# A soft mixture-of-experts tail: one tanh group moved ahead of an exponential, the combine product turned to 336 columns, the last logits stored slot by slot

## The chip, the cores and the metric

One Trainium2 chip, one of its cores. The metric is the device time of one execution in microseconds (us): three runs of the kernel before gave 433.04, 431.68 and 431.97, a median of 431.97 us. Everything is in float32, or in float32 split into two parts where a product is marked fp32r.

## The reference

Eight batches of 56 tokens (448 in all) of width 128. First a cross attention over 1500 context rows with 16 heads, then a soft mixture of experts with 64 experts of 32 slots each (2048 slots):

```python
x = x + xattn(layernorm(x), ctx, Wq, Wk, Wv, Wo)      # softmax over 1500 rows, 16 heads of 64
u = layernorm(x)
logits = (einsum('tzd,ed->tze', u, phi_w) + phi_b).reshape(8, 56, 64, 32)   # expert n, slot p
D = softmax(logits, axis=3)                           # dispatch: over the 32 slots of an expert
C = softmax(logits, axis=2)                           # combine: over the 64 experts of a slot
X = clip(einsum('tznp,tzd->npd', D, u), -33000, 65000)
X = tanh((X - mean(X)) * rsqrt(var(X) + 1e-5))
Y = einsum('npd,ndH->npH', X, expert_w) + expert_b[:, None, :]
x = x + einsum('tznp,npH->tzH', C, Y)
```

The einsum for `X` sums over all tokens. No expert's input is complete before the dispatch weights of every token are.

## The kernel before

The kernel is written with an engine program each for TensorE (PE), VectorE (DVE), ScalarE (ACT), GpSimd (POOL) and the DMA issuer SyncE (SP). Each engine runs its instructions in the order in which they are written, and waits on semaphores where the code says `wait_ge`. No scheduler moves anything.

The 448 tokens are four pairs of batches of 112 tokens (`q` = 0 to 3, `LAST` = 3). Attention takes most of the run. The softmaxes of pairs 0 to 2 are worked in beside it. The tail, some 50 us long, holds what needs the last pair.

The 2048 slots stand as 16 blocks of 128 (`k`, four experts each), and the tail walks through them in four quarters (`r`). The stages of a quarter are these:

- `slots_in`: PE adds up the experts' inputs of the quarter in a PSUM bank.
- `slot_stats` (DVE) clips and takes mean and variance. `slot_root` (POOL, four small instructions) makes the scale and the offset. `tanh_slots` (ACT) applies them.
- `turn_xt` (PE) transposes the quarter, `copy_xtT` (ACT) copies it out. `experts` (PE, 16 small products) multiplies by the expert weights. `add_expert_bias` (DVE) adds the bias and writes `yt`.
- `combine(0, r)` (PE) multiplies the turned combine weights `combT` of pairs 0 to 2 by `yt`: for each block three products, with the weights of one pair (112 columns) stationary and `yt` (128 columns) moving. `combine(1, r)` does the same for the last pair, after all else.

Between them stands the combine softmax of the last pair, which has its own chain. ACT copies the logits out of PSUM (`copy_logits`). DVE takes the maximum over the experts (`combine_max`). POOL subtracts it from the lower 32 experts, DVE from the upper 32 (`combine_shift_upper`). ACT takes the exponential of all 2048 columns (`combine_exp(LAST)`). DVE sums in two halves (`combine_sum_part`), takes the reciprocal and scales quarter by quarter (`combine_scale_quarter`). PE transposes (`turn_comb(LAST)`) and ACT copies to `combT`.

The logits of a token are stored with the slots innermost: column 32n + s for expert n and slot s. A maximum or a sum over the experts of one slot therefore reads with a step of 32 elements (128 bytes).

In the printed code below `by_expert` shapes the 2048 columns as 64 experts x 32 slots, `by_slot` as 32 x 64 with that step. `bank(k)` is one of the eight PSUM banks, `RING` the four through which transposes go. `tr` is a transpose on PE.

Of the kernel before, what the change touches and what calls it, by code (L numbers as in the profile page):

```python
# [5 lines left out]
F32 = mybir.dt.float32  # L6
# [6 lines left out]
def xattn_softmoe_kernel(  # L13
# [61 lines left out]
    with ExitStack() as ctx:  # L75
# [118 lines left out]
        comb = logit  # L194
        stats_at = [stat0_at, stat1_at, t0_at + KB8, t0_at + KB8 + 384]
# [10 lines left out]
        yt = at("yt", [128, NS, H], F32, t0_at)  # L206
        out_sb = at("out_sb", [PT, NQ, D], F32, oT_at + 2048)
# [123 lines left out]
        y2_pe = sem("y2_pe")  # L331
        out_dve = sem("out_dve")
# [92 lines left out]
        def _(pool):  # L425
# [121 lines left out]
            def combine_shift(q, n0=0, n1=N_EXP):  # L547
                pool.wait_ge(cmax_dve, q + 1)
                if q == LAST:
                    pool.wait_ge(last_dsub, LC)  # L550
# [72 lines left out]
            combine_shift(LAST, 0, N_EXP // 2)  # L623
# [5 lines left out]
        def _(pe):  # L629
# [381 lines left out]
            def turn_comb(q):  # L1011
                if q < LAST:
                    pe.wait_ge(comb_pool, q + 1)
                for r in range(4):
# [9 lines left out]
                    for c in range(4):  # L1024
                        k = 4 * r + c
                        last = tr(bank(RING[r])[:, PT * c:PT * c + PT], comb[q][:, 128 * k:128 * k + 128],
# [64 lines left out]
            def combine(part, r):  # L1091

                pe.wait_ge(yt_dve, max(r, part) + 1)
                q0, q1 = PARTS[part]
                for k in range(4 * r, 4 * r + 4):
                    for q in range(q0, q1):
                        last = mm(bank(SLOT_BANKS[part])[0:PT, H * (q - q0):H * (q - q0) + H],  # L1097
                                  combT[:, k, PT * q:PT * q + PT], yt[:, k, :],
                                  start=(k == 0 and q == q0), stop=(k == NS - 1), skip_group_check=True)
                if r == 3:  # L1100
                    last.then_inc(y2_pe, 1)

# [5 lines left out]
            combine(0, 0)  # L1108
            turn_xt(2)
            combine(0, 1)  # L1110
            experts(2)
            turn_xt(3)
            combine(0, 2)
            experts(3)
            turn_comb(LAST)
            combine(0, 3)
            for r in range(4):
                pe.wait_ge(combT_act, 12 + r + 1)
                combine(1, r)
# [3 lines left out]
        def _(act):  # L1123
# [68 lines left out]
            def copy_logits(q, c):  # L1192
                act.wait_ge(logit_pe, LC * q + c + 1)
                if q == LAST:
                    act.wait_ge(last_dsub, c + 1)
                nc.scalar.copy(logit[q][:, 512 * c:512 * c + 512],
# [152 lines left out]
            copy_xtT(1)  # L1349
            combine_exp(LAST)  # L1350
            tanh_slots(2)
# [3 lines left out]
            copy_combT(LAST)  # L1355


        @block.vector
        def _(dve):
# [124 lines left out]
            def combine_max(q):  # L1484
                dve.wait_ge(logit_act, LC * (q + 1))
                v.tensor_reduce(cmax[q][:, :], by_slot(logit[q][:, :]), AX.X, ALU.max).then_inc(cmax_dve, 1)
# [10 lines left out]
            def combine_sum_part(q, part):  # L1497
# [4 lines left out]
                if part:  # L1502
                    dve.wait_ge(csum_part, 6 if q == LAST else 2 * (q + 1))
# [167 lines left out]
            def combine_shift_upper(q):  # L1671

                half_n = slice(N_EXP // 2, N_EXP)
                dve.wait_ge(cmax_dve, q + 1)
                v.tensor_tensor(by_expert(comb[q][:, :])[:, half_n, :], by_expert(logit[q][:, :])[:, half_n, :],
                                cmax[q][:, :].unsqueeze(1).broadcast_to([PT, N_EXP // 2, P_SLOT]),
                                ALU.subtract).then_inc(csub_dve, 1)

            def combine_scale_quarter(q, r):

                dve.wait_ge(crec_dve, q + 1)
                part = by_expert(comb[q][:, QUARTER * r:QUARTER * r + QUARTER])
                v.tensor_tensor(part, part, csum[q][:, :].unsqueeze(1).broadcast_to([PT, N_EXP // 4, P_SLOT]),
# [58 lines left out]
```

## Time and profile before

| | kernel before |
|---|---|
| median of three runs | 431.97 us |
| the profiled execution, its own time | 429.94 us |
| its span in the trace | 428.2 us |
| PE busy in the span | 417.8 us (98%) |
| DVE / ACT / POOL busy | 335.8 / 245.0 / 170.1 us |
| granted TensorE clock | full in all 40 slices |

The span runs from the first to the last recorded event. The other 1.74 us of the execution's own time lie around it. Times in the trace count from the span's start. A row of the timeline gives the start, the time until its last instruction ended, and how many instructions it merges. Where instructions overlap in an engine's pipeline, the next row begins before the last one has ended. What an instruction holds the engine for is then the distance between starts.

A PE product of float32 appears as two MATMUL records, a transpose as one. So the twelve products of a `combine(0, r)` are 24 records. PE is busy 98% of the span, yet the tail has gaps. A wait on PE there is what the change can touch.

### The profile page before, as it was taken

The numbers are of one execution on the slowest core, as the hardware profiler recorded it, in microseconds if no ns is written. First come the engines' busy times: TensorE is split into PE (matmuls) and PEld (weight loads), VectorE is DVE, ScalarE is ACT, GpSimd is POOL, SyncE is SP. The second block draws the span as 40 slices with busy tenths as digits, with TensorE's granted clock in tenths as the row PEclk, the third lists the DMA queues.
The fourth block names the chain that finished last, engine by engine and source line by source line (L and its number), as shares of the span: only waits on it lengthen the run. The fifth ranks groups of instructions, "written<-read, shape, count | busy, mean of one in ns | idle before, by whom it ended". The sixth has DMA issues, their size and how long they took to land.

```text
span 428.2 us, 7420 instructions
## 1 busy us (share of the span) xinstructions
PE 417.8 (98%) x2973; PEld 383.4 (90%) x2973; DVE 335.8 (78%) x615; ACT 245.0 (57%) x412; POOL 170.1 (40%) x99
## 2 busy tenths in 40 slices
PE   7999999999999999999999999999999999999897
PEld 5888999999999999889999998899999888999787
DVE  4788756776886778767898689978988899669981
ACT  3577547664664546654673766466655564645541
POOL 5419701424450405032608053617146543456710
PEclk9999999999999999999999999999999999999999
DMA  7410110213020011110020001001000000396000
GB/s 197 144 27 10 41 51 14 63 43 96 14 48 38 20 14 18 69 18 14 14 73 20 12 14 72 21 12 15 0 20 12 2 12 20 54 259 181 2 2 23
DMA packets 15418, 19.05 MB, mean 44 GB/s; under 512 B 4032, under 2 KB 10960, under 8 KB 15384
## 3 DMA queue, kind: packets, MB, share of 16 engines
q1 hardware_dynamic: 15384, 18.57, 17.0%
q8 instruction: 24, 0.39, 0.4%
q14 instruction: 10, 0.08, 0.2%
HBM read 18.31 MB, written 0.26 MB: 43 GB/s over the span
## 4 chain that ended last, share of the span: by engine, by line
PE 73%; DVE 17%; ACT 7%; DMA 1%; issue 1%; SPq 0%; ACTq 0%
PE turned L735 14%; PE acc L755 8%; PE acc L757 7%; PE acc L756 7%; PE scores L719 7%; PE scores L725 7%; PE scores L722 7%; DVE small L1411 5%; DVE pT_l L1421 4%; ACT prob L1167 4%; PE misc L772 3%; PE misc L641 2%; PE scores L1097 2%; ACT pT_h L1160 1%; PE misc L800 1%; ACT logit L1218 1%
## 5 line engine op out<-in xcount | busy, mean ns | idle before, releaser
L1160 ACT CAST pT_h<-turned 125x512 fp32r<-125x512 f32 x168 | 95.2, 590 | 123.6 <-PE turned L735 122.9
L1421 DVE TENSOR_TENSOR pT_l<-turned,pT_h 125x512 fp32r<-125x512 f32 x168 | 112.4, 686 | 56.7 <-ACT pT_h L1160 55.9
L1411 DVE TENSOR_REDUCE small<-scores 128x1 f32<-128x500 f32 x168 | 107.9, 673 | 3.7 <-PE scores L725 3.3
L735 PE MATMUL turned<-ident,prob 128*125 128x128 f32 x672 | 94.4, 276 | 2.0 <-DVE pT_l L1421 1.7
L735 PEld LDWEIGHTS turned<-ident,prob 128*125 128x125 f32 x672 | 87.5, 187 | 9.7 <-DVE pT_l L1421 3.9
L755 PE MATMUL acc<-pT_h,ctx_nh 125*128 125x256 f32 (+1 forms) x288 | 95.0, 330 | 0.0
L1167 ACT ACTIVATE prob<-scores,small 128x1500 f32<-128x1500 f32 x56 | 84.9, 1517 | 10.9 <-DVE small L1414 10.7
L757 PE MATMUL acc<-pT_h,ctx_nl 125*128 125x256 f32 (+1 forms) x288 | 86.5, 300 | 0.0
L756 PE MATMUL acc<-pT_l,ctx_nh 125*128 125x256 f32 (+1 forms) x288 | 86.4, 300 | 0.0
L719 PE MATMUL scores<-ctx_th,qk_h 128*128 128x500 f32 x168 | 70.3, 419 | 0.4 <-ACT prob L1167 0.4
L725 PE MATMUL scores<-ctx_th,qk_l 128*128 128x500 f32 x168 | 65.3, 389 | 0.0
L722 PE MATMUL scores<-ctx_tl,qk_h 128*128 128x500 f32 x168 | 65.0, 387 | 0.0
L755 PEld LDWEIGHTS acc<-pT_h,ctx_nh 125*128 125x128 f32 x288 | 54.6, 190 | 0.7 <-issue 0.5
L756 PEld LDWEIGHTS acc<-pT_l,ctx_nh 125*128 125x128 f32 x288 | 54.6, 190 | 0.6 <-issue 0.5
L757 PEld LDWEIGHTS acc<-pT_h,ctx_nl 125*128 125x128 f32 x288 | 54.4, 189 | 0.0
L444 POOL TENSOR_TENSOR ctx_nh<-ctx_raw,zero 125x1536 fp32r<-125x1536 f32 x8 | 22.0, 2746 | 60.9 <-PE acc L757 60.5
L719 PEld LDWEIGHTS scores<-ctx_th,qk_h 128*128 128x128 f32 x168 | 31.6, 188 | 7.4 <-issue 2.1
L725 PEld LDWEIGHTS scores<-ctx_th,qk_l 128*128 128x128 f32 x168 | 31.5, 188 | 6.5
L722 PEld LDWEIGHTS scores<-ctx_tl,qk_h 128*128 128x128 f32 x168 | 31.7, 189 | 5.9 <-issue 1.4
L551 POOL TENSOR_TENSOR logit<-logit,cmax 112x2048 f32<-112x2048 f32 (+1 forms) x4 | 16.1, 4030 | 34.0 <-DVE cmax L1482 32.5
L448 POOL TENSOR_TENSOR ctx_nl<-ctx_raw,ctx_nh 125x1536 fp32r<-125x1536 f32 x8 | 28.0, 3497 | 0.6
L462 POOL TENSOR_TENSOR qk_h<-ahead,zero 128x896 fp32r<-128x896 f32 x6 | 10.1, 1680 | 30.7 <-PE scores L725 17.2
(212 smaller groups left out, 552.5 us busy)
## 6 DMA issues: line engine op xcount, KB each, us to landing
ctx_raw<-in_ctx_dram SPq DMA_DIRECT2D x7, 750.0 KB
rbc<-rden_row SPq DMA_DIRECT2D x15, 128.0 KB, 3.5
rbc<-rden_row SPq DMA_DIRECT2D x8, 192.0 KB, 3.0
eb<-in_L_ffn_expert_b_dram SPq DMA_DIRECT2D x4, 256.0 KB, 6.0
ctx_raw<-in_ctx_dram SPq DMA_DIRECT2D x3, 224.0 KB, 5.3
wq_sb<-in_L_xattn_Wq_dram SPq DMA_DIRECT2D x2, 256.0 KB, 4.6
wk_sb<-in_L_xattn_Wk_dram SPq DMA_DIRECT2D x2, 256.0 KB, 5.3
wv_sb<-in_L_xattn_Wv_dram SPq DMA_DIRECT2D x1, 512.0 KB, 3.6
```

What stands on the lines that cost most here:

```text
L448: gp.tensor_tensor(ctx_nl[a][:, :, :], ctx_raw[:, :, :], ctx_nh[a][:, :, :].bitcast(F32), ALU.subtract).then_inc(ctx_nat, 1)
L719: mm(o, hi, ctx_th[a][:, keys], start=True, stop=False)
L722: mm(o, hi, ctx_tl[a][:, keys], start=False, stop=False)
L725: mm(o, lo, ctx_th[a][:, keys], start=False, stop=True).then_inc(scores_pe, 1)
L735: last = tr(turned[0:CK, m, 128 * c:128 * c + 128], prob[u][:, CK * j:CK * j + CK], ident[:, :])
L755: mm(o, ctx_nh[a][:, j, :], hi, start=(j == 0), stop=False)
L756: mm(o, ctx_nh[a][:, j, :], lo, start=False, stop=False)
L757: last = mm(o, ctx_nl[a][:, j, :], hi, start=False, stop=(j == NC - 1))
L1160: nc.scalar.copy(pT_h[0:CK, PLACES[g // NT % 2][t], CPB * k:CPB * k + CPB, :], turned[0:CK, (KB * u + k) % 2, :].rearrange("p (c r) -> p c ...
L1167: nc.scalar.activation(prob[u][:, :].rearrange("p (k w) -> p k w", k=KB), scores[:, :, 0:KW], ACT.Exp, bias=negmax[:, u:u + 1], accum_out= ...
L1411: m = v.tensor_reduce(bankmax[:, u, k:k + 1], scores[:, k, 0:KW], AX.X, ALU.max)
L1421: v.tensor_tensor(pT_l[0:CK, place, dst, :], turned[0:CK, (KB * u + k) % 2, :].rearrange("p (c r) -> p c r", c=CPB), pT_h[0:CK, place, dst ...
```

## The change

It has four parts.

1. The logits of the last pair are stored by slot: column 64s + n instead of 32n + s. `copy_logits` writes with a step of 64 elements. The maximum, the two shifts and the sum then run along contiguous experts. Sum and maximum are one instruction each. The scaling reads with the step of 64 and writes the old order into `disp3`, from which PE transposes. POOL's shift loses its wait on `last_dsub`.
2. On ACT, `tanh_slots(2)` comes before `combine_exp(LAST)`. On DVE, `add_expert_bias(0)` comes before the upper shift.
3. `combine(r)` has `yt` stationary and the weights of three pairs (336 columns) moving: one product for each block instead of three. Its result is transposed, so an ACT copy to `y2T` and three PE transposes into bank M1 follow. The first three pairs' addition and store wait for them.
4. `combine_last` runs as `combine(1, r)` did. The three transposes stand between its second and third quarter.

```diff
-                nc.scalar.copy(logit[q][:, 512 * c:512 * c + 512], bank(...)[0:PT, :])   # q == LAST
+                    dst = logit[q][:, :].rearrange("p (s n) -> p n s", n=N_EXP)[:, EPB * c:EPB * c + EPB, :]
+                    src = bank(LOGIT_BANKS[q][c])[0:PT, :].rearrange("p (n s) -> p n s", s=P_SLOT)
+                    nc.scalar.copy(dst, src).then_inc(logit_act, 1)
...
+            def last_combine_shift_lower():
+                half_n = slice(0, N_EXP // 2)
+                by_slot = comb[LAST][:, :].rearrange("p (s n) -> p s n", n=N_EXP)[:, :, half_n]
+                pool.wait_ge(cmax_dve, LAST + 1)
+                gp.tensor_tensor(by_slot, by_slot, cmax[LAST][:, :].unsqueeze(2).broadcast_to([PT, P_SLOT, N_EXP // 2]),
+                                 ALU.subtract).then_inc(csub_pool, 1)
...
-                for k in range(4 * r, 4 * r + 4):
-                    for q in range(q0, q1):
-                        last = mm(bank(SLOT_BANKS[part])[0:PT, H * (q - q0):H * (q - q0) + H],
-                                  combT[:, k, PT * q:PT * q + PT], yt[:, k, :], ...)
+                for k in range(4 * r, 4 * r + 4):
+                    last = mm(bank(S0)[:, 0:LAST * PT], yt[:, k, :], combT[:, k, 0:LAST * PT],
+                              start=(k == 0), stop=(k == NS - 1))
...
+            def turn_y2():
+                pe.wait_ge(y2T_act, 1)
+                for q in range(LAST):
+                    last = tr(bank(M1)[0:PT, D * q:D * q + D], y2T[:, PT * q:PT * q + PT], ident[:, :])
+                last.then_inc(y2turn_pe, 1)
...
-            for r in range(4):
-                pe.wait_ge(combT_act, 12 + r + 1)
-                combine(1, r)
+            combine_last(0)
+            combine_last(1)
+            turn_y2()
+            combine_last(2)
+            combine_last(3)
...
+            act.wait_ge(y2_pe, 1)
+            nc.scalar.copy(y2T[:, :], bank(S0)[:, 0:LAST * PT]).then_inc(y2T_act, 1)
...
+                v.tensor_reduce(cmax[LAST][:, :], slot_rows(logit[LAST][:, :]), AX.X, ALU.max)     # one, contiguous
+                v.tensor_reduce(csum[LAST][:, :], slot_rows(comb[LAST][:, :]), AX.X, ALU.add)      # one, contiguous
+                src = comb[LAST][:, :].rearrange("p (s n) -> p n s", n=N_EXP)[:, EPB * r:EPB * r + EPB, :]
+                v.tensor_tensor(by_expert(comb_by_expert[LAST][:, QUARTER * r:QUARTER * r + QUARTER]), src,
+                                csum[LAST][:, :].unsqueeze(1).broadcast_to([PT, EPB, P_SLOT]), ALU.mult)
```

The order on ACT in the tail, from the tanh of the second quarter on (`logit_101` is the last pair's logits, which become its combine weights). Before:

```order
L1339 ACTIVATE xt<-xt,xt_nb,xt_rs 128x128 [waits nb_pool]
L1339 ACTIVATE xt<-xt,xt_nb,xt_rs 128x128 x3
L1344 COPY xtT<-turned 128x512 [waits xtT_pe] x2
L1218 ACTIVATE logit_101<-logit_101 112x2048 [waits csub_dve,csub_pool]
L1339 ACTIVATE xt<-xt,xt_nb,xt_rs 128x128 [waits nb_pool]
L1339 ACTIVATE xt<-xt,xt_nb,xt_rs 128x128 x3
L1344 COPY xtT<-scores 128x512 [waits xtT_pe]
```

And now:

```order
L1368 ACTIVATE xt<-xt,xt_nb,xt_rs 128x128 [waits nb_pool]
L1368 ACTIVATE xt<-xt,xt_nb,xt_rs 128x128 x3
L1373 COPY xtT<-turned 128x512 [waits xtT_pe] x2
L1368 ACTIVATE xt<-xt,xt_nb,xt_rs 128x128 [waits nb_pool]
L1368 ACTIVATE xt<-xt,xt_nb,xt_rs 128x128 x3
L1247 ACTIVATE logit_101<-logit_101 112x2048 [waits csub_dve,csub_pool]
L1373 COPY xtT<-scores 128x512 [waits xtT_pe]
```

The exponential of 2048 columns stands behind the third tanh group now, but still ahead of the copy of that quarter's transpose.

On DVE, from the third quarter's statistics to the scaling. Before:

```order
L1663 BN_AGGR xt_mv<-xt_st 128x2 x3
L1675 TENSOR_TENSOR logit_101<-logit_101,cmax_112 112x1024 [waits cmax_dve]
L1668 TENSOR_TENSOR yt<-scores,eb 128x512 [waits yt_pe,eb_in]
L1668 TENSOR_TENSOR yt<-acc,eb 128x512 [waits yt_pe]
...
L1500 TENSOR_REDUCE cmax_112<-logit_101 112x32 [waits cexp_act]
L1500 TENSOR_REDUCE half_stat<-logit_101 112x32 [waits cexp_act]
L1504 TENSOR_TENSOR cmax_112<-cmax_112,half_stat 112x32 [waits csum_part]
L1506 RECIPROCAL cmax_112<-cmax_112 112x32 [waits csum_dve]
L1668 TENSOR_TENSOR yt<-misc,eb 128x512 [waits yt_pe]
L1683 TENSOR_TENSOR logit_101<-logit_101,cmax_112 112x512 [waits crec_dve] x4
```

And now:

```order
L1703 BN_AGGR xt_mv<-xt_st 128x2 x3
L1708 TENSOR_TENSOR yt<-scores,eb 128x512 [waits yt_pe,eb_in]
L1715 TENSOR_TENSOR logit_101<-logit_101,cmax_112 112x32x32 [waits cmax_dve]
L1708 TENSOR_TENSOR yt<-acc,eb 128x512 [waits yt_pe]
...
L1524 TENSOR_REDUCE cmax_112<-logit_101 112x32 [waits cexp_act]
L1526 RECIPROCAL cmax_112<-cmax_112 112x32 [waits csum_dve]
L1708 TENSOR_TENSOR yt<-misc,eb 128x512 [waits yt_pe]
L1722 TENSOR_TENSOR disp_104<-logit_101,cmax_112 112x512 [waits crec_dve] x4
```

The first bias addition has passed the upper shift, the sum is one instruction, and the scaling writes `disp_104` (`disp3`).

On PE, the end of the program. Before:

```order
L1097 MATMUL scores<-yt,combT 112x128 [waits yt_dve]
L1097 MATMUL scores<-yt,combT 112x128 x11
L1097 MATMUL acc<-yt,combT 112x128 [waits yt_dve,combT_act]
L1097 MATMUL acc<-yt,combT 112x128 x3
L1097 MATMUL acc<-yt,combT 112x128 [waits yt_dve,combT_act]
L1097 MATMUL acc<-yt,combT 112x128 x3
L1097 MATMUL acc<-yt,combT 112x128 [waits yt_dve,combT_act]
```

And now:

```order
L1105 MATMUL scores<-combT,yt 128x336 [waits yt_dve]
L1105 MATMUL scores<-combT,yt 128x336 x3
L1114 MATMUL acc<-yt,combT 112x128 [waits combT_act]
L1114 MATMUL acc<-yt,combT 112x128 x3
L1114 MATMUL acc<-yt,combT 112x128 [waits combT_act]
L1114 MATMUL acc<-yt,combT 112x128 x3
L1123 MATMUL misc<-ident,y2T 112x128 [waits y2T_act]
L1123 MATMUL misc<-ident,y2T 112x128 x2
L1114 MATMUL acc<-yt,combT 112x128 [waits combT_act]
```

Twelve products of 128 columns have become four of 336, and three transposes stand inside the last pair's combine.

## Rows read from the trace of the kernel before

**Rows 1.** Chain that ended last, tail: start us, us, what.
```profile
405.42 1.91 ACT logit L1218
407.33 1.55 ACT xt L1339 x4
...
412.27 1.05 PE misc L1087 x32
...
413.35 0.70 DVE yt L1668
...
414.09 2.88 PE scores L1097 x24
...
417.98 0.92 PE turned L1026 x8
...
425.81 0.29 DVE out_sb L1712
```
**Rows 2.** Timeline, PE: start us, us, line, operation, count [idle before].
```profile
402.69 1.08 PE L1087 MATMUL scores<-ew,xtT 128*32 128x128 f32 x32
...
409.02 0.63 PE L1078 MATMUL scores<-ident,xt 128*128 128x128 f32 x4 [0.16 <-ACT xt L1339]
409.48 2.79 PE L1097 MATMUL scores<-yt,combT 128*112 128x128 f32 x24
```
**Rows 3.** Timeline, DVE, 398 to 406 us.
```profile
398.07 3.72 DVE L1486 TENSOR_REDUCE cmax<-logit 112x32 f32<-112x2048 f32 x1
401.71 0.69 DVE L1655 TENSOR_SCALAR xt<-misc 128x512 f32<-128x512 f32 x1
...
403.63 1.69 DVE L1675 TENSOR_TENSOR logit<-logit,cmax 112x1024 f32<-112x1024 f32 x1
405.25 0.68 DVE L1668 TENSOR_TENSOR yt<-scores,eb 128x512 f32<-128x512 f32 x1
405.85 0.67 DVE L1668 TENSOR_TENSOR yt<-acc,eb 128x512 f32<-128x512 f32 x1
```
**Rows 4.** Timeline, POOL, 398 to 406 us.
```profile
398.37 0.24 POOL L566 TENSOR_SCALAR xt_nb<-xt_mv 128x4 f32<-128x4 f32 x1
...
400.09 0.20 POOL L571 TENSOR_TENSOR xt_nb<-xt_nb,xt_rs 128x4 f32<-128x4 f32 x1
401.87 2.37 POOL L551 TENSOR_TENSOR logit<-logit,cmax 112x1024 f32<-112x1024 f32 x1 [1.58 <-DVE cmax L1486]
404.33 1.09 POOL L566 TENSOR_SCALAR xt_nb<-xt_mv 128x4 f32<-128x4 f32 x1
```
**Rows 5.** Groups by line and shape: count | busy us, mean ns | idle before.
```profile
L1472 DVE TENSOR_REDUCE dmax<-logit 112x32 f32<-112x1024 f32 x4 | 4.7, 1207 | 0.0
L1478 DVE TENSOR_REDUCE cmax<-logit 112x32 f32<-112x1024 f32 x2 | 4.0, 1976 | 0.0
...
L1683 DVE TENSOR_TENSOR logit<-logit,cmax 112x512 f32<-112x512 f32 x4 | 2.5, 683 | 0.0
...
L1506 DVE RECIPROCAL cmax<-cmax 112x32 f32<-112x32 f32 x2 | 0.7, 354 | 0.1
...
L531 POOL TENSOR_TENSOR disp<-logit,dmax 112x2048 f32<-112x2048 f32 x3 | 10.9, 3648 | 23.7 <-DVE dmax L1472 23.7
```
**Rows 6.** Groups by line and shape, PE: eight float32 products of 512 columns.
```profile
L800 PE MATMUL misc<-phiT,xnT 128*112 128x512 f32 x16 | 8.2, 592 | 0.0
```
**Rows 7.** Timeline, ACT, 387 to 393 us.
```profile
387.09 0.63 ACT L1212 ACTIVATE disp<-disp 112x512 f32<-112x512 f32 x1 [2.80 <-DVE disp L1526]
387.63 0.57 ACT L1196 COPY logit<-turned 112x512 f32<-112x512 f32 x1
...
392.71 0.63 ACT L1212 ACTIVATE disp<-disp 112x512 f32<-112x512 f32 x1 [1.05 <-DVE disp L1526]
```
**Rows 8.** DMA issues of the output: count, KB, us from issue to landing.
```profile
out_dram<-out_sb SPq DMA_DIRECT2D x1, 168.0 KB, 2.6
...
out_dram<-out_sb SPq DMA_DIRECT2D x1, 56.0 KB, 1.6
```

More of the change, by code:

```diff
@@ L331, in xattn_softmoe_kernel @@
         y2_pe = sem("y2_pe")
+        y2T_act = sem("y2T_act")
+        y2turn_pe = sem("y2turn_pe")
         out_dve = sem("out_dve")
@@ L1025, in turn_comb @@
                         k = 4 * r + c
-                        last = tr(bank(RING[r])[:, PT * c:PT * c + PT], comb[q][:, 128 * k:128 * k + 128],
+                        last = tr(bank(RING[r])[:, PT * c:PT * c + PT], comb_by_expert[q][:, 128 * k:128 * k + 128],
                                   ident[0:PT, 0:PT])
@@ L1089, in experts, with combine, combine_last @@
                 last.then_inc(yt_pe, 1)
-            def combine(part, r):
-                pe.wait_ge(yt_dve, max(r, part) + 1)
-                q0, q1 = PARTS[part]
+            def combine(r):
+                pe.wait_ge(yt_dve, r + 1)
                 for k in range(4 * r, 4 * r + 4):
-                    for q in range(q0, q1):
-                        last = mm(bank(SLOT_BANKS[part])[0:PT, H * (q - q0):H * (q - q0) + H],
-                                  combT[:, k, PT * q:PT * q + PT], yt[:, k, :],
-                                  start=(k == 0 and q == q0), stop=(k == NS - 1), skip_group_check=True)
+                    last = mm(bank(S0)[:, 0:LAST * PT], yt[:, k, :], combT[:, k, 0:LAST * PT],
+                              start=(k == 0), stop=(k == NS - 1))
                 if r == 3:
                     last.then_inc(y2_pe, 1)
+            def combine_last(r):
+                pe.wait_ge(combT_act, 12 + r + 1)
+                for k in range(4 * r, 4 * r + 4):
+                    last = mm(bank(ACC)[0:PT, 0:H], combT[:, k, LAST * PT:TOK], yt[:, k, :],
+                              start=(k == 0), stop=(k == NS - 1))
+                if r == 3:
+                    last.then_inc(y2_pe, 1)
+            def turn_y2():
[3 more added lines that the diff above has]
+                last.then_inc(y2turn_pe, 1)
             pe.wait_ge(ew_in, 16)
@@ L1349, in _ @@
             copy_xtT(1)
+            tanh_slots(2)
             combine_exp(LAST)
-            tanh_slots(2)
             copy_xtT(2)
@@ L1482, in combine_max_part, with slot_rows, last_combine_max, last_combine_sum @@
                     v.tensor_tensor(cmax[q][:, :], cmax[q][:, :], half_stat[:, :], ALU.max).then_inc(cmax_dve, 1)
-            def combine_max(q):
-                dve.wait_ge(logit_act, LC * (q + 1))
-                v.tensor_reduce(cmax[q][:, :], by_slot(logit[q][:, :]), AX.X, ALU.max).then_inc(cmax_dve, 1)
+            def slot_rows(ap):
+                return ap.rearrange("p (s n) -> p s n", n=N_EXP)
+            def last_combine_max():
+                dve.wait_ge(logit_act, LC * (LAST + 1))
+                v.tensor_reduce(cmax[LAST][:, :], slot_rows(logit[LAST][:, :]), AX.X, ALU.max).then_inc(cmax_dve, 1)
+            def last_combine_sum():
+                dve.wait_ge(cexp_act, LAST + 1)
+                v.tensor_reduce(csum[LAST][:, :], slot_rows(comb[LAST][:, :]), AX.X, ALU.add).then_inc(csum_dve, 1)
+                dve.wait_ge(csum_dve, LAST + 1)
+                v.reciprocal(csum[LAST][:, :], csum[LAST][:, :]).then_inc(crec_dve, 1)
             def dispatch_sum(q, part):
@@ L1502, in combine_sum_part @@
                 if part:
-                    dve.wait_ge(csum_part, 6 if q == LAST else 2 * (q + 1))
+                    dve.wait_ge(csum_part, 2 * (q + 1))
                     v.tensor_tensor(csum[q][:, :], csum[q][:, :], half_stat[:, :], ALU.add).then_inc(csum_dve, 1)
```

52 lines of the change are left out of this document (26 added, 26 removed).

## The prediction

> **What bounds the kernel now.** I read the chain of waits first, from 400 us to the end. It holds what the end waits for: PE from 409.02 us on, broken once by the third bias addition, and ahead of that ACT and DVE [rows 1, 2]. Only the tail is changed, so only the tail can pay. The chain's middle is the place to look at. The exponential of the combine weights runs 405.42 to 407.33, and only then the third tanh group (1.55 on the chain), for which PE waits until 409.02 [rows 1, 2]. From there PE has work behind work: combine, experts, four transposes, and one more gate. The third bias addition (413.35, 0.70) must end before the third combine quarter can start at 414.09 [rows 1]. That start, which I call the gate, is the coordinate of my sum. Behind it stand two combine quarters of the first three pairs, one experts quarter, the sixteen transposes of the last weights and the last pair's combine, whose end releases DVE at 425.81 [rows 1]. Whatever moves the gate, or what is shorter behind it, moves the end by as much, if nothing else becomes late.
>
> Second I read the timelines of DVE and POOL from 398 to 406 us, since they feed that gate. DVE's maximum holds it from 398.07 to 401.71, 3.64 us. POOL's shift starts after it at 401.87 and takes 2.37, and DVE's upper shift takes 1.69 [rows 3, 4]. The first bias addition starts at 405.25, though its experts were done at 402.69 + 1.08 = 403.77 [rows 2, 3]. It stood behind the upper shift on DVE.
>
> **Part 1, the layout.** A maximum over 1024 columns takes 1.207 us where they are contiguous, 1.976 with the step of 128 bytes [rows 5]. 2048 columns took 3.72 with the step [rows 3], so a column costs (3.72 - 1.976)/1024 = 1.70 ns there. A contiguous column costs at most 1.207/1024 = 1.18 ns, and 0.95 if the fixed part of the strided rows (1.976 - 1.744 = 0.23) is taken off; I take 1.04, between them. The contiguous maximum then takes 1.207 + 1024 x 1.04 ns = 2.28, holding DVE for 2.20: from 398.07 to 400.27. Bounds: 2.1 and 3.64. Statistics of the third quarter hold DVE for 403.63 - 401.71 = 1.92 [rows 3] and end at 402.2. DVE then waits for the first experts. Their end does not move, since PE, ACT and POOL ahead of them are unchanged. The first bias addition starts at 403.77 + 0.08 = 403.85.
>
> From there DVE is the chain:
> - first bias addition, 405.85 - 405.25 = 0.60 [rows 3]: to 404.45;
> - upper shift. 512 columns of such a subtraction or product take 0.683 [rows 5]; 1024 take that plus 512 x 1.04 ns = 1.22. Before it took 1.69, but POOL's shift ran until 404.24 [rows 4], and from there to DVE's end at 405.32 [rows 3] it is 1.08. I take 1.15; bounds 1.08 and 1.69: to 405.60;
> - second bias addition 0.60: to 406.20;
> - statistics of the last quarter 1.92, plus the 0.09 until their last end: 408.21;
> - POOL's root. In the profile it runs 398.37 to 400.29 [rows 4], 1.92, and starts some 0.2 behind the statistics: 2.14: 410.35;
> - the tanh group 1.64 and 0.05 to start: 412.04; PE 0.14 later: 412.18;
> - PE's four transposes hold it 409.48 - 409.02 = 0.46 [rows 2]: the gate at 412.64.
>
> It stood at 414.09, so the gate moves by -1.45. PE itself would be ready earlier. Its first combine quarter can start at about 404.65, behind the second experts, and with 2.26 for a quarter (below), 0.46 for transposes and 1.0 for experts it is free at 410.7. PE idles some 1.4 us there, and the work is not late.
>
> The copies of the logits get a step of 256 bytes on ACT's writes. No row shows a strided write on ACT. Bounds: the 0.57 of now [rows 7], and 0.57 + 512 x (1.70 - 1.04) ns = 0.91 if ACT suffers as DVE does. I take 0.75. All of that is covered. Each copy starts 0.54 behind its exponential [rows 7], and with c for a copy the fourth exponential could start at 387.63 + 3c + 2 x 0.54, which passes its 392.71 [rows 7] only for c above 1.33.
>
> The Trainium skill ("Advanced Engine Details and Errata", SBUF Cachelines) says that an access of another 16-byte line each time pays a penalty. By this rule the change buys its contiguous reductions with steps in five other places, the four scalings and the copies; for DVE's reads the trace agrees, 1.976 against 1.207.
>
> The scalings read with the step now. Each held DVE some 0.60 of its 0.683 [rows 5]; with 512 x 0.66 ns more, 0.95. Four of them, from about 411.7, end at 415.5. PE wants the first when its third combine and fourth experts are over, at 412.64 + 2.26 + 1.05 = 415.95. They are covered, with 0.45 us to spare for the last and more for the ones before. Without that cover every 0.1 us on each would cost 0.4.
>
> **Part 2, the order.** The tanh group now needs POOL's root of the third quarter. POOL's shift starts at 400.45 (0.08 behind the maximum's end at 400.37) and now subtracts one value for 32 contiguous columns, as the dispatch shift does: 3.648 for 2048 columns, 1.9 for 1024; the row of the same half now says 2.37 [rows 4, 5]. Both bounds stay. The root follows by 1.92 + 0.09 and ends at 404.36 or 404.83. DVE's upper shift starts at 404.45. This is a race. POOL's small instruction at 404.33 took 1.09 where its like took 0.24, exactly while DVE had its own upper shift [rows 4, 3]. If POOL loses, the root ends at about 405.9.
>
> The Trainium skill ("SBUF — State Buffer", Who interferes with whom) calls it an exclusive lock between a DVE instruction with two SBUF inputs and a GpSimd one that reads SBUF. By this rule the loser stands still for the whole 1.15, and the trace agrees with 1.09 against 0.24.
>
> If POOL wins, tanh ends at 406.0, the exponential at 407.9, and DVE, busy with statistics until 408.2, sums (2.20), inverts (0.354 and 0.05, [rows 5]) and adds the third bias at 410.9, behind the experts. It is not late. If POOL loses: tanh to 407.6, exponential 1.91 [rows 1] to 409.45, sum to 411.65, reciprocal to 412.05, third bias to 412.8, gate 412.84. The loss is 0.2. The exponential hides behind the statistics in the one case and is nearly late in the other.
>
> **Part 3, 336 columns.** Twelve products are 24 records in 2.79, a record lasting about 0.275: (2.79 - 0.275)/23 = 0.109 from start to start, 2.62 a quarter [rows 2]. Records of 512 columns come in pairs that last 2 x 8.2/16 = 1.02, one of them 0.592 [rows 6]: 0.43 from start to start. So 336 columns: 0.109 + 208 x (0.43 - 0.109)/384 = 0.283. Eight records: 2.26. The saving is 0.36 a quarter; bounds 0 (the wide product brings nothing) and 0.5 (against the 2.88 of [rows 1]). Two quarters stand behind the gate: -0.72. The three transposes cost 3 records at about 0.92/8 = 0.115 [rows 1]: +0.33. Their copy (336 columns, less than the 0.57 of 512 [rows 7]) lies under two quarters of the last pair's combine, 1.75 us.
>
> **Sum.** -1.45 - 0.72 + 0.33 = -1.84 if POOL wins, -1.64 if it loses. I take -1.75. Against the profiled execution: 429.94 - 1.75 = 428.2. The median of the runs is 431.97, 2.03 above it, and I carry the difference over to it: 430.2.
>
> **The stores.** The first store is released by the transposes now, and leaves some 0.2 ahead of where it stood; the second leaves 1.8 earlier. A whole combine of the last pair stood between them, 32 records at 0.109, 3.5 us, and the first landed within 2.6 [rows 8]. Now it is half of that, 1.75, and the first is still in flight when the second leaves. In the sum the second keeps its 1.6.
>
> **Rivals.**
> - *The locks cost more.* POOL's shift takes 2.37 and DVE's upper shift 1.69: the gate stands 0.5 later and the loss of the race is added, -1.84 + 0.7 = -1.14: 430.8. For: both rows stand so today. Against: they were measured while colliding with each other, which the new order takes apart. Chance 0.10.
> - *The wide product is no cheaper*: PE is 2.62 a quarter whatever the shape. -1.84 + 0.72 = -1.12: 430.85. For: no float32 row of 336 columns. Against: [rows 6]. Chance 0.08.
> - *The second store waits for the first.* It lands 2.6 after its issue instead of 1.6: -0.75: 431.2. For: three times the bytes ahead of it. Against: the small store's 1.6 is mostly a fixed time, and the bigger one needs only 1.0 more. Chance 0.10.
> - *The layout does nothing*: contiguous sums of this shape cost as strided ones. The sum of the weights then starts at 409.5 and holds 3.7, and the gate stands at 414.35: +0.26 - 0.72 + 0.33 = -0.1: 431.85. Against: [rows 5]. Chance 0.04.
> - *Slower: ACT's strided writes.* A copy taking c above 1.33 delays the fourth exponential by 3c - 4.0, and all of the tail with it. At c = 1.9 the gain is gone; at 2.6 (5 ns a column) it is +3.8 - 1.75 = +2.05: 434.0. For: no row has such a write. Against: DVE's strided reads cost 1.7 ns a column, a third of it. Chance 0.07.
>
> **How the numbers follow.** Forecast 0.61, the rivals 0.39 together. A difference of 0.3% is 1.3 us, about what a measurement of this kernel can tell from no change. The forecast's own values, -1.64 to -1.84, stand only 0.4 from that line, and I give 0.04 of its 0.61 to the near side. Faster: 0.57, 0.03 of the locks, and 0.02 of the stores, 0.62. Same: 0.04 + 0.07 + 0.08 + 0.08 + 0.04 = 0.31. Slower: 0.07. The range: downward the unknowns are the wide product's 0.5 and a start of PE at 410.7 instead of 412.2, with scatter of the runs of 0.3: 429.0. Upward it takes in locks, product, stores and layout: 431.8. Outside lie the strided write and some 0.08 below.
>
> **What would show it.** The maximum at 2.3 us and the sum likewise, without a strided one. The first bias addition at 403.85. The last tanh group at 410.4, PE waiting for it by 1.2 to 1.5 us, and its next combine quarter at 412.6. The wide records 0.28 apart. The logits copies under 0.95. The last output addition at 424.0. I am wrong if the gate stands elsewhere because the exponential or a lock is on the chain, or if a logits copy takes over 1.33.

## The result and the profile after

| | before | after |
|---|---|---|
| median of 13 runs each | 431.39 us | 428.93 us |
| ratio, 95% interval | | 0.9943 (0.9927 to 0.9958) |
| profiled execution, own time / span | 429.94 / 428.2 us | 429.79 / 428.0 us |
| first score product in the trace | 11.74 us | 13.57 us |
| first slot statistics in the trace | 394.31 us | 396.17 us |
| first slot statistics to the span's end | 33.89 us | 31.83 us |

The change made the kernel faster by 0.57%, 2.46 us between the medians; the interval spans 1.8 to 3.15 us. I had forecast 1.75 us, 430.2 us, in a range from 429.0 to 431.8. The median lies 0.07 us below the range. The interval holds 2.0 us as well as 2.46, and 1.75 lies just outside it.

The two spans, 428.2 and 428.0, hide the gain. This execution of the changed kernel started badly. Its first score product came 1.83 us later than that of the kernel before, and it carried the delay to the tail (1.86 us). The chain of its first microseconds shows what happened (start us, us, what):

```profile
2.64 5.44 DMA ctx_raw<-in_ctx_dram
8.08 0.14 issue
8.21 0.92 PE misc L651 x4
9.14 0.51 PE turned L679
...
9.87 0.21 PE turned L679
...
13.57 0.49 PE scores L729
```

The kernel before, same view:

```profile
2.64 4.77 DMA ctx_raw<-in_ctx_dram
...
8.48 0.11 PE turned L669
...
11.74 0.49 PE scores L719
```

The context landed 0.67 us later, and then each product of two weight blocks (L679, before L669) took 0.21 where it had taken 0.10 to 0.11. The busy time by stretches of the changed kernel's profile (us, PE, PEld, DVE, ACT, POOL busy, then PEclk, DMA share, GB/s) gives the reason:

```profile
0.00:8.00 8.00, 4.41 (x15) 3.10 (x15) 2.40 (x12) 1.87 (x2) 3.62 (x12) 1.00 0.69 198
8.00:12.00 4.00, 3.79 (x24) 3.07 (x25) 1.79 (x4) 1.17 (x2) 3.02 (x3) 0.57 0.74 194
12.00:16.00 4.00, 3.99 (x25) 3.32 (x25) 2.87 (x6) 1.75 (x4) 3.92 (x2) 1.00 0.58 183
```

The first stretch of the kernel before, same view:

```profile
0.00:8.00 8.00, 5.25 (x19) 3.52 (x19) 2.78 (x13) 1.87 (x2) 3.52 (x12) 1.00 0.75 204
```

The granted clock was 0.57 on average from 8 to 12 us, so TensorE ran at the lower of its two levels, 1.2 GHz, for most of it. Ahead of it PE had been busy 4.41 of 8 us, where it was busy 5.25 in the kernel before, whose clock stayed at 1.00. Such a start isn't a property of the change: 9 of the 72 runs of the kernel before that were made beside the experiments have a mean clock of 0.996 to 0.998 too, the mean of this profile being 0.996.

The tail must therefore be read from a mark of its own. I take the first slot statistics on DVE. The mark in the kernel before, and in the changed kernel:

```profile
394.31 0.63 DVE L1655 TENSOR_SCALAR xt<-scores 128x512 f32<-128x512 f32 x1
...
396.17 0.63 DVE L1695 TENSOR_SCALAR xt<-scores 128x512 f32<-128x512 f32 x1
```

The timeline of the changed kernel's tail (start us, us, engine, line, operation):

```profile
399.93 2.25 DVE L1520 TENSOR_REDUCE cmax<-logit 112x32 f32<-112x2048 f32 x1
...
402.26 1.92 POOL L562 TENSOR_TENSOR logit<-logit,cmax 112x1024 f32<-112x1024 f32 x1
...
405.76 0.69 DVE L1708 TENSOR_TENSOR yt<-scores,eb 128x512 f32<-128x512 f32 x1 [1.66 <-PE scores L1097]
405.98 0.20 POOL L581 TENSOR_TENSOR xt_nb<-xt_nb,xt_rs 128x4 f32<-128x4 f32 x1
406.21 1.65 ACT L1368 ACTIVATE xt<-xt,xt_nb,xt_rs 128x128 f32<-128x128 f32 x4 [0.98 <-POOL xt_nb L581]
406.37 1.22 DVE L1715 TENSOR_TENSOR logit<-logit,cmax 112x1024 f32<-112x1024 f32 x1
...
407.77 1.90 ACT L1247 ACTIVATE logit<-logit 112x2048 f32<-112x2048 f32 x1
...
410.02 2.25 DVE L1524 TENSOR_REDUCE cmax<-logit 112x32 f32<-112x2048 f32 x1
410.19 0.23 POOL L576 TENSOR_SCALAR xt_nb<-xt_mv 128x4 f32<-128x4 f32 x1 [4.01 <-DVE xt_mv L1703]
...
412.14 1.65 ACT L1368 ACTIVATE xt<-xt,xt_nb,xt_rs 128x128 f32<-128x128 f32 x4 [2.01 <-POOL xt_nb L581]
...
413.42 3.92 DVE L1722 TENSOR_TENSOR disp<-logit,cmax 112x512 f32<-112x512 f32 x4
...
413.94 0.63 PE L1088 MATMUL scores<-ident,xt 128*128 128x128 f32 x4 [1.19 <-ACT xt L1368]
...
414.40 2.43 PE L1105 MATMUL scores<-combT,yt 128*128 128x336 f32 x8
...
416.76 1.08 PE L1097 MATMUL misc<-ew,xtT 128*32 128x128 f32 x32
...
419.36 2.44 PE L1105 MATMUL scores<-combT,yt 128*128 128x336 f32 x8
421.63 1.91 PE L1114 MATMUL acc<-yt,combT 128*112 128x128 f32 x16
...
425.65 0.29 DVE L1754 TENSOR_TENSOR out_sb<-x_sb,acc 112x128 f32<-112x128 f32 x1 [1.19 <-PE acc L1114]
```

The maximum takes 2.25 us where it took 3.72 [rows 3], POOL's shift 1.92 where it took 2.37 [rows 4]. The upper shift takes 1.22 where it took 1.69 [rows 3]; that is the order's doing and not the layout's, since it takes 1.22 in the kernel with the order only, too. DVE waits 1.66 for the first experts. The third combine quarter starts at 414.40, 18.23 us behind the mark; before it was 414.09 - 394.31 = 19.78 [rows 1]. PE waits 1.19 us for the last tanh group.

### The profile page after: what moved, and what is told of

Its sections match the earlier page's. It is cut to its first block, busy times and chain, and to the rows that moved or that the text cites. A ratio compares the mean times of both kernels' runs of the same rounds, so it can differ in the third digit from the quotient of the medians.

```text
span 428.0 us, 7292 instructions
## 1 busy us (share of the span) xinstructions
PE 417.5 (98%) x2912; PEld 380.0 (89%) x2912; DVE 333.5 (78%) x613; ACT 247.1 (58%) x413; POOL 168.8 (39%) x99
## 4 chain that ended last, share of the span: by engine, by line
PE 73%; DVE 16%; ACT 7%; DMA 1%; POOL 1%; issue 1%; SPq 0%; POOLq 0%; DVEq 0%
PE turned L745 14%; PE acc L765 8%; PE acc L767 7%; PE acc L766 7%; PE scores L729 7%; PE scores L735 7%; PE scores L732 7%; DVE small L1442 5%; DVE pT_l L1452 4%; ACT prob L1192 4%; PE misc L782 3%; PE misc L651 2%; ACT pT_h L1185 1%; PE misc L810 1%; DMA ctx_raw<-in_ctx_dram 1%; PE scores L1105 1%
## 5 line engine op out<-in xcount | busy, mean ns | idle before, releaser
L553 POOL TENSOR_TENSOR logit<-logit,cmax 112x2048 f32<-112x2048 f32 x3 | 13.8, 4588 | 32.5 <-DVE cmax L1513 32.5
```

## The experiments

Each kernel with an interval ran 6 to 12 times, on the same chip as the kernel before, whose medians beside them were 431.44 (first four kernels of the table), 431.18 (next four) and 431.34 us (last). The other two have a single run each, so only their traces are used. The last column is the time from the first slot statistics to the end of the span, which I call the tail. The trace gives spans to 0.1 us, so a tail is good to 0.05.

| kernel | median us | ratio (95% interval) | tail us |
|---|---|---|---|
| before again | 431.31 | 1.0004 (0.9986 to 1.0021) | 33.87 |
| change again | 428.82 | 0.9942 (0.9919 to 0.9964) | 31.87 |
| wide product only | 430.55 | 0.9970 (0.9952 to 0.9989) | 33.10 |
| layout and order only | 429.66 | 0.9951 (0.9933 to 0.9969) | 32.23 |
| order only | 433.12 | 1.0045 (1.0021 to 1.0070) | 35.46 |
| layout only | 430.01 | 0.9970 (0.9947 to 0.9992) | 32.18 |
| change with the old order | 428.67 | 0.9939 (0.9917 to 0.9962) | 31.20 |
| change, logits copied twice | 430.00 | 0.9969 (0.9949 to 0.9988) | 31.89 |
| change, exponential first (ACT) | 429.47, one run | | 33.56 |
| change, upper shift first (DVE) | 430.32, one run | | 31.34 |
| old order, second quarter split | 428.27 | 0.9938 (0.9921 to 0.9955) | 30.91 |

**Both kernels again.** No edit.

> The kernel before, unchanged. It tells two places for the surplus of the measured change (-2.46 us of medians against -1.75 forecast and -2.02 between the first bias statistics and the last output addition of the two traces). Theory S (scatter of the start): the time from the first slot statistics to the end of the span is again 33.9 us within 0.1, and only the time before it differs from 394.31 us, by up to 2 us either way. Theory H (the head of the program is faster after the change, for instance through code loading): the head is longer here than in every run of changed kernels by some 0.4 us.

> The changed kernel, unchanged. Theory S: 31.8 us from the first slot statistics to the end of the span, within 0.1, against 33.9 before; its head falls among those of the kernel before; the medians of the same rounds differ by 2.0 us, give or take 0.6. Theory H: heads shorter by 0.4, medians 2.4 to 2.5 apart.

The tails came out at 33.87 and 31.87, within 0.04 of the first profiles. Read without the spans, from the mark to the start of the last output addition, the two pairs of traces differ by 31.50 - 29.48 = 2.02 and 31.51 - 29.50 = 2.01 us. From the first score product to the first slot statistics it took 382.57 and 382.60 us in the first pair of traces, 382.54 and 382.53 in the second. The head is the same in both programs, and only its start differs, at 11.6 to 13.6 us in these four. That is as theory S has it. The medians were again 2.5 us apart (431.31 and 428.82), more than the 2.0 of the tails, with an interval that still holds 2.0.

**The wide product alone.** It has parts 3 and 4 of the change on the kernel before. The diff is cut to the product.

```diff
...
-                    for q in range(q0, q1):
-                        last = mm(bank(SLOT_BANKS[part])[0:PT, ...], combT[:, k, PT * q:PT * q + PT], yt[:, k, :], ...)
+                    last = mm(bank(S0)[:, 0:LAST * PT], yt[:, k, :], combT[:, k, 0:LAST * PT], ...)
...
```

> Only the product of 336 columns, its copy, its transposes and the stores as changed; layout and order are those of before. My sum: the gate (start of the third combine quarter) stays 19.8 us behind the first slot statistics, each quarter of the first three pairs holds PE for 2.26 instead of 2.62, transposes cost 0.33: -0.4 us. Rival (a wide product is no cheaper): +0.33 us. Since the layout of before has a wait of PE on the third bias addition, the quarters ahead of it gain nothing.

The tail was 33.10, a gain of 0.78, twice my sum (0.73 at the start of the last output addition). The gate moved too: 413.42 against a mark of 394.00 is 19.42, 0.36 earlier. PE's own work stood ahead of the third bias addition there, so a shorter second combine brought the third experts, the bias and the gate forward. So the sentence of my expectation that the quarters ahead gain nothing was wrong. The rest is 0.34 and 0.36 for the two quarters less 0.33 for the transposes, as forecast for the change.

**Layout and order without the wide product.** The diff is cut as above.

```diff
...
-                    last = mm(bank(S0)[:, 0:LAST * PT], yt[:, k, :], combT[:, k, 0:LAST * PT], ...)
+                    for q in range(q0, q1):
+                        last = mm(bank(SLOT_BANKS[part])[0:PT, ...], combT[:, k, PT * q:PT * q + PT], yt[:, k, :], ...)
...
```

> Layout and order as changed, but twelve products of 128 columns a quarter and no transposes of the result, as before. My sum: the gate moves by the whole 1.45 to 1.55 us, and so does the end: -1.5 us. PE is busy 0.36 longer in each of the two quarters ahead of the gate, which its idle 1.2 us there covers. Rival (the wide product also pays ahead of the gate, by starting the third transposes sooner): only -1.2.

The tail was 32.23, a gain of 1.65. The gate stood 413.62 - 395.37 = 18.25 behind the mark, as in the change, so the wide product brings nothing ahead of it here. The other 0.1 lies in the quarter behind the gate. It held PE 2.71 (413.62 to 416.33) instead of 2.80 (414.09 to 416.89). The kernel before, behind its gate at 414.09 [rows 1]:

```profile
416.89 1.08 PE L1087 MATMUL misc<-ew,xtT 128*32 128x128 f32 x32
...
419.49 2.79 PE L1097 MATMUL scores<-yt,combT 128*112 128x128 f32 x24
422.12 3.66 PE L1097 MATMUL acc<-yt,combT 128*112 128x128 f32 x32
```

And this kernel, with its wait at the turn:

```profile
413.15 0.63 PE L1088 MATMUL scores<-ident,xt 128*128 128x128 f32 x4 [0.49 <-ACT xt L1353]
413.62 2.78 PE L1107 MATMUL scores<-yt,combT 128*112 128x128 f32 x24
```

Here a quarter whose first product waited for its operand is 0.09 slower, and with the layout the wait is at the turn, ahead of it.

**Order only.** The two swaps of the change on the kernel before.

```diff
+            tanh_slots(2)
             combine_exp(LAST)
-            tanh_slots(2)
...
-            combine_shift_upper(LAST)
             dve.wait_ge(eb_in, 16 * EPT)
             add_expert_bias(0)
+            combine_shift_upper(LAST)
```

> Only the order as changed (third tanh group ahead of the exponential on ACT, first bias addition ahead of the upper shift on DVE); layout by expert and twelve products as before. My sum: maximum still strided, so DVE comes to the first bias addition at 403.85 and to the upper shift at 404.45 (times of the profile of before); the root's small instructions meet the upper shift and end near 407.2, tanh to 408.9, exponential only then to 410.7, strided sums to 414.8, reciprocal 0.4, third bias addition 0.7: gate 415.8 instead of 414.09, so 1.7 us slower than before (35.6 us from the first slot statistics to the end). Rival (the order is worth something by itself, since the tanh group and the turn are earlier): some 0.5 us faster than before.

It was slower by 1.6 us in the tail (35.46, expected 35.6) and by 0.45% in the runs. The timeline shows the race lost and the exponential late:

```profile
404.55 1.22 DVE L1675 TENSOR_TENSOR logit<-logit,cmax 112x1024 f32<-112x1024 f32 x1
404.65 1.19 POOL L567 TENSOR_SCALAR xt_var<-xt_mv 128x4 f32<-128x4 f32 x1
...
408.84 1.90 ACT L1218 ACTIVATE logit<-logit 112x2048 f32<-112x2048 f32 x1
...
410.77 1.94 DVE L1500 TENSOR_REDUCE cmax<-logit 112x32 f32<-112x1024 f32 x1 [2.49 <-ACT logit L1218]
...
415.75 2.88 PE L1097 MATMUL scores<-yt,combT 128*112 128x128 f32 x24 [1.83 <-DVE yt L1668]
```

POOL's small instruction took 1.19 instead of 0.23 while DVE shifted. The exponential stood behind the tanh group, DVE waited 2.49 for it, and PE 1.83 for the third bias addition behind the sums. The rival, a gain of 0.5, did not occur.

**Layout only.** Here the old order of ACT and DVE stands on the new layout. The diff is against the kernel with layout and order.

```diff
-            tanh_slots(2)
             combine_exp(LAST)
+            tanh_slots(2)
...
             slot_stats(2)
+            last_combine_shift_upper()
             dve.wait_ge(eb_in, 16 * EPT)
             add_expert_bias(0)
-            last_combine_shift_upper()
```

> Only the layout as changed; order and products as before. My sum: the shorter maximum frees DVE at 400.3, the upper shift runs at 402.4 to 403.5 in the gap in which DVE otherwise waits for the first experts, the sum ends at 409.5, and the gate stands at 412.2 behind PE's own work and the third bias addition: 1.9 us faster than before, 32.0 us from the first slot statistics to the end, 0.2 better than layout and order together (32.23). Rival (the order is what brings the gain, as its place in the change suggests): the exponential ahead of the tanh group holds PE up, and the gain is under 1.0.

The tail was 32.18: 1.70 faster than before, 0.2 less than my sum, since the gate stood 414.52 - 396.42 = 18.10 behind the mark and not 412.2 - 394.31 = 17.89. It equals layout and order together (32.23). With the twelve products of 128 columns, the order brought nothing on top of the layout, and cost nothing.

**The change with the old order.** It is the same edit on the changed kernel.

> The changed kernel with the order of before on ACT and DVE: exponential ahead of the third tanh group, upper shift ahead of the first bias addition. My sum: gate at 411.75, two quarters shorter by 0.35 to 0.45 each, transposes 0.33: 2.8 us faster than before, 31.1 us from the first slot statistics to the end, 0.75 better than the change. Rival (the order carries the gain): slower than the change, 32.5 or more.

The tail was 31.20, 0.65 better than the change (31.85) and 0.1 from my sum. Its timeline:

```profile
402.55 1.24 DVE L1715 TENSOR_TENSOR logit<-logit,cmax 112x1024 f32<-112x1024 f32 x1
...
403.88 1.91 ACT L1247 ACTIVATE logit<-logit 112x2048 f32<-112x2048 f32 x1
...
404.30 0.69 DVE L1708 TENSOR_TENSOR yt<-scores,eb 128x512 f32<-128x512 f32 x1 [0.52 <-PE scores L1097]
...
411.45 0.69 DVE L1708 TENSOR_TENSOR yt<-misc,eb 128x512 f32<-128x512 f32 x1 [1.18 <-PE misc L1097]
411.55 0.63 PE L1088 MATMUL scores<-ident,xt 128*128 128x128 f32 x4 [0.17 <-ACT xt L1368]
...
412.20 2.53 PE L1105 MATMUL scores<-combT,yt 128*128 128x336 f32 x8
```

The upper shift fills the gap in which DVE waits for the first experts (0.52 is left of 1.66), and PE waits 0.17 for the last tanh group instead of 1.19. Between the medians the step is 0.15, which the runs cannot tell from nothing. The tails can: those of an unchanged kernel repeated within 0.04.

**Each logits copy twice.**

```diff
+                    nc.scalar.copy(spare, src)          # an unused place, the same step
                     nc.scalar.copy(dst, src).then_inc(logit_act, 1)
```

> The changed kernel with each of the four copies of the last logits made twice, first into an unused place with the same step. One copy holds ACT for 0.86 in the changed kernel. By my formula (a delay of 3c - 4.0 for c above 1.33) two of them, c = 1.72, delay the fourth exponential and the first slot statistics by 1.15 us, with nothing lost behind it: 1.1 slower than the change. Rival A (the copies are hidden wholly): no change. Rival B (they lie on the path all along): 4 x 0.86 = 3.4 slower, and then the change itself already loses 4 x 0.35 there.

In the changed kernel a copy holds ACT 390.34 - 389.48 = 0.86 (four exponentials in 394.57 - 388.94 = 5.63). The last part with the doubled copies:

```profile
388.75 0.63 ACT L1244 ACTIVATE disp<-disp 112x512 f32<-112x512 f32 x1 [2.81 <-DVE disp L1569]
389.29 1.05 ACT L1225 COPY junk<-turned 112x512 f32<-112x512 f32 x1
...
390.14 1.10 ACT L1226 COPY logit<-turned 112x512 f32<-112x512 f32 x1
...
395.54 0.65 ACT L1244 ACTIVATE disp<-disp 112x512 f32<-112x512 f32 x1
```

From the first to the fourth exponential it is 6.79, 1.16 more, and the tail behind the mark is unchanged at 31.89. The formula 3c - 4.0 holds: 1.15 was expected, and the medians, 430.00 and 428.82, lie 1.2 apart (1.4 if each is taken against its own kernel before, 431.18 and 431.44). The single strided copy, 0.86, stays under the 1.33 and costs nothing.

**Only ACT's order, only DVE's order.** One half of the edit above each, on the changed kernel.

> The changed kernel with the order of before on ACT alone: exponential ahead of the third tanh group, while the upper shift stays behind the first bias addition on DVE. My sum: the upper shift ends at 405.6 in the times of the profile of before, the exponential runs to 407.55, tanh to 409.1, the turn at 409.2, experts to 413.0, gate 413.8: 33.1 us from the first slot statistics to the end, against 31.85 for the change. Rival (the ACT order is what costs the change its 0.65 against the old order): 31.2.

> The changed kernel with the order of before on DVE alone: upper shift ahead of the first bias addition; tanh stays ahead of the exponential. My sum: the shift fills DVE's gap, statistics of the last quarter end 1.0 earlier, tanh no longer holds PE, but the exponential ends 1.3 later than with the old order, at 408.8, and with it the sum (411.1), reciprocal (411.5) and third bias addition: gate 412.25, 31.65 us. Rival (DVE's order alone carries the 0.65): 31.2.

The tails were 33.56 and 31.34. With the exponential first and the shift late, ACT holds the tanh group back behind a shift that is itself behind the bias addition, 1.7 worse than the change. I had expected 1.25 worse; the gate stands 413.96 - 394.14 = 19.82 behind the mark, expected 413.8 - 394.31 = 19.49. With the upper shift first, 0.5 of the 0.65 is had without touching ACT. I had expected 0.2 of it. The exponential was late, and DVE waited for it:

```profile
411.54 2.29 DVE L1524 TENSOR_REDUCE cmax<-logit 112x32 f32<-112x2048 f32 x1 [1.38 <-ACT logit L1247]
```

The sum starts 411.54 - 397.16 = 14.38 behind the mark, 1.45 later than with the old order on both engines (407.63 - 394.70 = 12.93). But there the third bias addition still waited 1.18 for the experts, and that wait covers most of it: the bias addition comes only 0.22 later (414.13 - 397.16 = 16.97 against 411.45 - 394.70 = 16.75).

**The version that follows.** Old order, and on PE half of the second combine quarter behind the third experts. The diff is cut to PE.

```diff
...
             turn_xt(2)
-            combine(1)
+            combine(1, 0, 2)
             experts(2)
+            combine(1, 2, 4)
             turn_xt(3)
...
```

> The change with the old order on both engines, and the second combine quarter in two halves around the third experts on PE: two blocks before them cover the copy, two behind them cover the third bias addition, for which PE idles 0.2 to 0.3 and starts slowly in the version with the old order (31.20 us). My sum: PE without a gap to the third combine quarter, 0.4 us better: 30.8 us from the first slot statistics to the end, 3.1 us faster than the kernel before. Rival (the experts then wait for the copy of their transpose, 0.8 us behind the turn, since half a quarter, 1.13 us, covers it only barely): no better than 31.2.

```profile
407.83 1.30 PE L1105 MATMUL scores<-combT,yt 128*128 128x336 f32 x4
409.06 1.08 PE L1097 MATMUL misc<-ew,xtT 128*32 128x128 f32 x32
...
410.07 1.40 PE L1105 MATMUL scores<-combT,yt 128*128 128x336 f32 x4
410.21 0.69 DVE L1709 TENSOR_TENSOR yt<-misc,eb 128x512 f32<-128x512 f32 x1
...
411.43 0.63 PE L1088 MATMUL scores<-ident,xt 128*128 128x128 f32 x4
...
411.90 2.43 PE L1105 MATMUL scores<-combT,yt 128*128 128x336 f32 x8
```

PE has no gap from the third turn to the third combine, and the third bias addition lies under the second half. The half quarter behind the experts took 1.40 and the one ahead of them 1.30, though no wait is shown before it. So the slow start of a quarter doesn't need a wait. The tail is 30.91, 0.94 better than the change and 2.96 better than before. The median, 428.27, is the lowest of all, but its interval overlaps those of the change and of its old-order twin.

## Why the prediction was wrong

The mechanisms were right and the sum was too small: 1.75 us, where the two pairs of traces give 2.02 and 2.01 behind the mark (2.06 and 2.00 with the rounded spans), and the medians 2.46.

- **The maximum and the first bias addition.** 2.20 us of hold were forecast, 402.10 - 399.93 = 2.17 came. The bias addition starts 405.76 - 396.17 = 9.59 behind the mark, forecast 403.85 - 394.31 = 9.54.
- **The chain to the gate.** The upper shift held DVE 1.13 (forecast 1.15), statistics 1.92. Behind them I charged POOL's root 2.14, and it ended 2.00 behind the statistics. In the row that I took it from, POOL had still been busy with the root of the quarter ahead, and started 0.22 behind the statistics; free, it starts 0.08 behind them. The gate moved by 1.55 instead of 1.45. This is the one term of it that was mis-sized.
- **The wide product.** 2.26 a quarter were forecast, and the second of the two came in 2.27. The first held PE 416.76 - 414.40 = 2.36, but it had been 2.80 before and not 2.62. The 0.09 of a quarter behind a wait went with the wait; I had named the 2.88 as a bound and summed without it. Both 2.26 and 2.62 are also about 0.1 too low for a quarter that experts follow (2.36 in the change, 2.71 with layout and order only). That this cancels in the difference is luck.
- **The race.** POOL's root ended at 406.18, DVE's upper shift started at 406.37. POOL won by 0.19, where I saw 0.09 (404.45 - 404.36). Halving the loss cost the forecast another 0.1.
- **The transposes** cost 0.33, as forecast, and their copy was hidden. **The stores**: the first landed within 2.2 us, the second within 1.6. That rival did not occur.
- **ACT's strided writes.** 1.03 to 1.06 us were measured, above my upper bound of 0.91. I had taken DVE's cost of a strided read for ACT's write. They stayed under the limit of 1.33 by their hold of 0.86, and the doubled copies show that the limit was right.
- **The scalings** read with the step. The four take 3.92 as a row, of which the last alone takes 1.06, so each of the others holds DVE (3.92 - 1.06)/3 = 0.95, as forecast; they stayed covered.

These corrections give 1.84 + 0.10 + 0.09 = 2.03, which is what the traces show behind the mark. The last 0.4 us to the medians is not in the tail. The eight other kernels with an interval have medians between 0.5 below and 0.4 above the 431.3 of the kernel before plus the difference of their tails and, with the doubled copies, of their exponentials. The change itself lies 0.4 to 0.5 below in both its measurements, the doubled copies 0.5 below, the old-order twin at 0.0.

Two parts of a run's time lie outside the tail. The first is what lies outside the span. In 116 runs of kernels that keep the old product and its stores it is 1.86 us on average, and in 28 of them 1.9 to 2.3. In 60 runs of kernels with parts 3 and 4 it is 1.80 and never above 1.84. So about 0.07 of the 0.4 goes with parts 3 and 4, by what cause no run shows.

The second is the time ahead of the mark. The spans less the tails make it 395.62 us on average in 84 runs of the kernel before and 395.17 in 20 runs of the change, with standard errors of 0.11 and 0.17. It holds the rest. A faster head (theory H) would show between the first score product and the first slot statistics, and that is 382.5 to 382.6 us in eleven of the thirteen traces, of either program. In the other two (layout only, and the doubled copies without their 1.16) it is 0.6 and 0.4 more, all of it between 55 and 72 us. DVE waits there for the landing of a DMA, 2.08 and 1.91 us against 0.47 to 1.66 in the other traces. Layout only:

```profile
64.12 0.67 DVE L1460 TENSOR_TENSOR oT<-acc,rbc 128x384 f32<-128x384 f32 x1 [2.08 <-DMA rbc<-rden_row]
```

Both programs have that wait, and the first score product starts at 11.5 to 14.5 us in both. So the traces name no cause that is the change's own, and chance in which starts the runs drew remains. It isn't shown: the 0.45 us between the two averages is about twice its standard error.

The step that failed is the carrying over to the median, with a scatter of 0.3 us for the range, beside the sizes. I took 431.97, a median of three runs whose neighbours reach from 429.58 to 433.62, as if it were known; over 13 runs it is 431.39, which is 0.58 lower. The forecast of 430.22 missed 428.93 by 1.29: 0.58 by this, 0.27 because the tail gained 2.02 and not 1.75, and 0.44 that is not in the tail. With the first two mended it gives 429.4, which lies inside the range; the last 0.44, whose cause stays open, is what put the median 0.07 below it. Nor was the lower bound worked out: the unknowns named for it, 2 x (0.50 - 0.36) = 0.28 for the product, 1.5 for PE's start and 0.3 of scatter, make 2.1 us together and not the 1.2 that the range took.

What I did not see at all is that part 2 of the change works against part 1. My sum followed the new order only, and noted that PE would idle 1.4 us at the third turn without asking what the old order would do with the freed DVE time. Layout alone gives 1.70, order alone costs 1.6, and the change with the old order is 0.65 better than the change. With twelve products the two orders tie (32.23 and 32.18), because PE's own work reaches almost to the gate there: even with the new order PE waits only 0.49 for the tanh group. Once part 3 has shortened that work, the wait is 1.19 with the new order and 0.17 with the old. So part 2 works against parts 1 and 3 together.

## What to carry to other kernels

When an edit frees an engine, work out the old order as well as the new one on the shortened timeline. Here the swap stopped filling a gap that the first edit had opened. Read a change in the tail from a mark at its beginning, since the start of each execution scatters by more than the change. A duration taken from a row holds only with that row's neighbours: what was queued ahead of it (POOL's 0.14), whether its first operand was waited for (PE's 0.09), and what follows it (PE's 0.1). A median of three runs was 0.58 off that of thirteen, a third of the forecast gain.

## What the runs showed of the hardware

- A copy on ACT from PSUM to SBUF of 112x512 float32 took 0.57 us with contiguous writes and 1.03 to 1.06 with a write step of 256 bytes, and held ACT 0.86 us (1.04 to 1.10 with the copies doubled).
- A float32 maximum or sum on DVE over 2048 contiguous columns took 2.25 us against 3.72 for a step of 128 bytes; a product with one operand read at a step of 256 bytes held DVE 0.95 a quarter of 512 columns, against 0.60 with it read contiguously.
- Two float32 records of 336 columns a block: eight held PE 2.27 us, and 2.36 with experts behind them; the 24 records of 128 columns that do the same work held 2.63 and 2.71 in the same places, each 0.09 to 0.10 more where a wait came first (2.46, 2.80).
- DVE and POOL held each other up. A POOL instruction of 0.23 took 1.19 while a two-input DVE instruction of 1.22 ran (order only). The other way, DVE's upper shift took 1.69 in the kernel before, where POOL's shift lay over its first 0.61 (403.63 to 404.24), and 1.22 in order only, with the same layout, where POOL's shift had ended before it.
- The scatter between executions lies in their first 72 us: the first score product starts at 11.5 to 14.5 us, a DMA's landing near 62 us is waited for 0.47 to 2.08, and behind 72 us the traces run in step. In the profile of the changed kernel the context landed 0.67 us later than before, and at a granted clock of 0.57 from 8 to 12 us another 1.2 us was lost; everything behind ran 1.83 us later, to the tail. A late landing is not enough for it: in the doubled copies' trace the context landed at 7.65 and the clock was 0.57 too, in the old-order twin's it landed at 7.74 and the clock was 1.00.
